# Masking the diagonal exponentials on GpSimd instead of the transposed scores on TensorE, in a causal attention stage

## The reference, cut to what matters

```python
x = x + 0.5 * ffn(layernorm(x))      # 16 experts of 176, top 4, and a shared one of 704
x = x + attention(layernorm(x))      # this case is about this stage
x = x + 0.5 * ffn(layernorm(x))

# attention: 32 query heads, 8 key/value heads, head width 8, rotary positions
scores = jnp.einsum('bhqd,bhkd->bhqk', q, k_rep) / scale
scores = jnp.where((kpos > qpos)[None, None], -jnp.inf, scores)
attn = jax.nn.softmax(scores, axis=-1)
out = jnp.einsum('bhqk,bhkd->bhqd', attn, v_rep)
```

## Time and profile before

| | |
|---|---|
| median of 3 runs | 797.16 us (796.89 to 799.98) |
| the profiled execution | 796.24 us |
| its span, first to last instruction | 794.4 us |
| PE, DVE, ACT, POOL busy over the span | 93%, 58%, 47%, 24% |
| the attention's scores and products | about 283 to 549 us of the span |

### The profile page before, as it was taken

The page is one execution under the profiler, slowest core; times in us unless marked ns, Lnnn a source line. Parts: engine busy times, 40 slices in busy tenths (PEclk is TensorE's granted clock), DMA queues, the critical chain, the costliest instruction groups (busy, mean ns, idle before and its releaser), DMA issues.

```text
span 794.4 us, 13291 instructions
## 1 busy us (share of the span) xinstructions
PE 735.7 (93%) x4776; PEld 391.3 (49%) x4776; DVE 460.9 (58%) x942; ACT 373.9 (47%) x569; POOL 189.7 (24%) x158
## 2 busy tenths in 40 slices
PE   4699999999996677999999999997879999999997
PEld 2356666656564233333333434543446656556665
DVE  6555454545548977899988877643533333333334
ACT  6434343333334466746657667776622222222222
POOL 1273333333344412000000000000143333333332
PEclk9999999999998689999999999999699999999999
DMA  5353333334310000000000000000042222221212
GB/s 170 101 148 112 119 119 113 113 120 133 116 54 1 0 1 1 1 1 1 1 2 1 1 1 2 1 1 1 2 112 77 67 65 72 60 79 53 79 53 80
DMA packets 16169, 44.37 MB, mean 56 GB/s; under 512 B 2658, under 2 KB 5090, under 8 KB 16132
## 3 DMA queue, kind: packets, MB, share of 16 engines
q1 hardware_dynamic: 12388, 33.65, 14.4%
q10 hardware_dynamic: 3744, 10.23, 3.9%
HBM read 42.68 MB, written 1.19 MB: 55 GB/s over the span
## 4 chain that ended last, share of the span: by engine, by line
PE 82%; DVE 6%; issue 4%; ACT 4%; DMA 2%; POOL 1%; SPq 1%; DVEq 0%; ACTq 0%; POOLq 0%
PE psum L857 53%; PE psum L1021 8%; PE psum L1005 8%; PE psum L994 7%; PE psum L992 2%; PE psum L1008 2%; DVE m_part L807 2%; PE psum L979 1%; ACT kT L563 1%; PE psum L1028 1%; DMA coef_dram<-oT 1%; POOL R L379 1%; DVE kaug L797 1%; DMA R<-coef_dram 1%; DMA x_res<-x_dram 1%
## 5 line engine op out<-in xcount | busy, mean ns | idle before, releaser
L857 PE MATMUL psum<-xT,W_hi 128*128 128x512 f16 x880 | 265.2, 383 | 0.0
L379 POOL TENSOR_TENSOR R<-R 128x512 f32<-128x512 f32 x112 | 152.5, 1363 | 298.0 <-DVE R L718 250.1
L807 DVE TENSOR_REDUCE m_part<-psum 128x1 f32<-128x512 f32 (+3 forms) x384 | 188.1, 550 | 42.3 <-PE psum L994 40.1
L704 DVE SCALAR_TENSOR_TENSOR R<-psum,R 128x512 f32<-128x512 f32 x108 | 74.7, 691 | 226.0 <-ACT R L491 225.9
L491 ACT ACTIVATE R<-psum 128x512 f32<-128x512 f32 x108 | 64.4, 597 | 265.5 <-PE psum L857 265.5
L857 PE MATMUL psum<-W_hi,R 128*128 (+1 forms) x896 | 166.5, 275 | 11.5 <-DVE R L718 11.5
L578 ACT ACTIVATE R<-psum 128x1024 f32<-128x1024 f32 x144 | 141.8, 1024 | 68.1 <-PE psum L1005 45.6
L857 PE MATMUL psum<-xT,W_lo 128*128 128x512 f16 x440 | 168.2, 382 | 0.0
L857 PEld LDWEIGHTS psum<-xT,W_hi 128*128 (+1 forms) x880 | 86.8, 99 | 83.4 <-issue 3.5
L857 PE MATMUL psum<-W_lo,R 128*128 (+1 forms) x448 | 123.3, 275 | 0.0
L994 PE MATMUL psum<-kT,qT 128*128 128x512 f16 (+3 forms) x384 | 105.8, 334 | 1.0 <-DVE m_part L807 0.6
(11 more groups left out here) (101 smaller groups left out, 457.3 us busy)
## 6 DMA issues: line engine op xcount, KB each, us to landing
R<-coef_dram SPq DMA_DIRECT2D x64, 256.0 KB, 3.8
w_stage<-w_dram ACTq DMA_DIRECT2D x26, 384.0 KB, 2.9
R<-coef_dram SPq DMA_DIRECT2D x8, 448.0 KB, 3.5
R<-coef_dram SPq DMA_DIRECT2D x8, 384.0 KB, 3.4
R<-coef_dram SPq DMA_DIRECT2D x8, 320.0 KB, 3.5
R<-coef_dram SPq DMA_DIRECT2D x8, 192.0 KB, 3.7
x_res<-x_dram SPq DMA_DIRECT2D x8, 128.0 KB, 2.2
R<-coef_dram SPq DMA_DIRECT2D x8, 128.0 KB, 3.1
```

Of the source, the lines that this page charges most:

```text
L379: nc.gpsimd.tensor_tensor(hc[:, c, :], v[:, j, c, :], C[:, j, c * CH:(c + 1) * CH], ALU.mult).then_inc(s_hc[c], 1)
L704: nc.vector.scalar_tensor_tensor(out=v[:, j, c, :], in0=bank[2 + c][:, :], scalar=1.0 / WS, in1=sg[:, c, :], op0=ALU.mult, op1=ALU.mult).t ...
L807: nc.vector.tensor_reduce(m_part[:, h, kc:kc + 1], ps[:, 0:n], axis=AX.X, op=ALU.max).then_inc(free_of(e), 1)
L857: ins = nc.tensor.matmul(o, stat(a, k), mov(b, k), start=first and n == 0, stop=last and n == 3 * k_parts - 1, **kw)
```

## The change

Line 1008 goes: the transposed scores on the diagonal get no mask. GpSimd gets 32 operations, one for each pair of the 16 diagonal steps, that write zero over the forbidden entries of the exponentials in place. They stand behind the eight bias additions in its program. The diagonal step's `pv` waits for the two of its unit. The planner's cost of a diagonal `st` loses 0.45 on PE and gains 2.5 on GpSimd, so that it writes another order. The mask of the plain scores (line 992) stays.

```diff
         if kind == "st":
             diag = e[5] == ORDER[e[6]]
-            return [(PE, 0.9 if diag else 0.45), (ACTE, 0.95)], [("q2", e[3]), ("st", e[1] - 1, e[2])]
+            return [(PE, 0.45), (ACTE, 0.95)] + [(POOL, 2.5)] * diag, [("q2", e[3]), ("st", e[1] - 1, e[2])]
...
+        s_select = sem("s_select")
...
                 nc.gpsimd.tensor_tensor(x_res[:, t, :], x_res[:, t, :], bias[:, QKV:QKV + D],
                                         ALU.add).then_inc(s_xb, 1)
+
+            for e in events:
+                if e[0] == "st" and e[5] == ORDER[e[6]]:
+                    n, pair = e[1], e[2]
+                    pool.wait_ge(s_exp, 2 * n + pair + 1)
+                    own = prob[:, n % 2, 2 * pair:2 * pair + 2, :].rearrange("p g (j q) -> p (g j) q", q=P)
+                    nc.gpsimd.affine_select(out=own, in_=own, pattern=[[0, 2 * GQ], [1, P]], compare_op=ALU.is_ge,
+                                            fill=0.0, base=0, channel_multiplier=-1).then_inc(s_select, 1)
             low_parts(2)
...
                         ins = nc.tensor.matmul(bank[gl], kT[:, gh * GLO + gl, kt * P:(kt + 1) * P],
-                                               qT2[:, u % 4, :, :], start=True, stop=kt != t)
-                        if kt == t:
-                            ins = nc.tensor.matmul(bank[gl].rearrange("p (j n) -> p j n", j=GQ), identb[:],
-                                                   maskb[:, 1, :].unsqueeze(1).to_broadcast([P, GQ, P]),
-                                                   start=False, stop=True)
+                                               qT2[:, u % 4, :, :], start=True, stop=True)
                     ins.then_inc(s_st, 1)
...
                     pe.wait_ge(s_exp, 2 * n + 2)
+                    if kt == t:
+                        pe.wait_ge(s_select, 2 * (u + 1))
```

## The result

The changed kernel takes 811.83 us (median of 4, 810.75 to 812.35) against 797.77 for the kernel before; the ratio is 1.0167, 95% interval 1.0148 to 1.0185. It is 13 to 14 us slower. The forecast was 801, the range 789 to 813. The sign was right and the size under a third of the real one (0.5% against 1.67%).

The account below looks back on a forecast made before the run. TensorE was taken to bound the attention, VectorE close behind. Masks -13.0, first wait +6.5, other selects +0.5 and +7.5, VectorE +3.5 gave +5.0 on 796.24: 801 us, range 789 to 813.

Parts of the forecast that it names:

- What VectorE takes back: Between 301 and 530 us, TensorE's reduced work brings it close to VectorE's pace: +3.5 us, between 0 and 9.5.
- seven to eighteen: Plain scores counted between a diagonal step's scores and product in units 1 to 10, said to cover the select waits.
- The select's price: One GpSimd select over 1024 fp32 elements per partition: taken as 1.8 us, between 0.9 and 2.7.
- a sign of being wrong: The prediction said it would be wrong if the selects were below 1.1 us.
- dear selects: Rival: selects on GpSimd cost 2.5 to 2.7 us, as for two reads; 812.5 us, +16; chance 0.25.
- The first wait: Product of n = 2 waits for selects queued behind GpSimd's eight bias additions: +6.5 us.
- s: GpSimd's time for one select, taken as 1.8 us.
- Units 1 to 10 covered, 11 to 15 short of 7.5 us: Select waits at diagonal products: hidden in units 1 to 10 but for +0.5 us at unit 10; +7.5 in 11 to 15.
- the formula: Time needed from a diagonal step's first scores to its product, 1.15 + 2s, set against TensorE's work in that stretch.
- Masks at 13.0 us: Dropping the diagonal mask matmuls on TensorE, 60 of 64 counted as saving at 0.216 us each: -13.0 us.
- masks off the path: Rival: VectorE's reduces pace the stretch and 9.5 us is given back; +11, 807 us; chance 0.08.
- TensorE's 98.8%: TensorE busy 98.8 of 100 us between 350 and 450, taken as evidence that it bounds the attention.

Follow-up runs that it names:

- the halved reduces: VectorE's plain-score reduces over half their columns, masks in, no selects: 791.35 us in the order of before, 802.15 us in the new order.
- the two other lists: The changed kernel with the bias additions behind the selects of n = 5 and the planner told 1.1 or 0 us for a select: 800.48 and 794.19 us.
- 0 in the planner: The changed kernel, bias additions behind the selects of n = 5, planner told 0 us for a select instead of 2.5: 794.19 us, ratio 0.9963.
- the kernel without selects: The kernel before, in its old order, with line 1008's masks left out and nothing in their place: 793.65 us, ratio 0.9949.
- the kernel with selects: The changed kernel with the planner's old costs, so the old order, masks out and selects in: 800.48 us, ratio 1.0027.
- the kernel with the additions behind: The changed kernel, same order, with the eight GpSimd bias additions moved behind the selects of n = 5: 806.52 us, ratio 1.0105.

## Why the prediction was wrong

- **The new order, which stood in the sum with nothing of its own.** This is the step that failed. "What VectorE takes back: +3.5 us" was to hold all that the planner's new list does, and it counted only sums of work over 228 us. It held two things. The first, masks that bring less because VectorE stands next to TensorE: in the changed kernel's order they brought 11 us and not 13.0, which the term covers. The second, the new list itself: 18.8 us with masks in, 12 without. I had even used the crowding as a benefit: the "seven to eighteen" plain scores before a diagonal product were what hid the select. I did not ask what the steps look like from which they were taken. Part of the answer stood in the trace of before, where in units 6 to 9 steps with three and with six plain scores take nearly the same time.
- **The select's price.** I took 1.8 us between 0.9 and 2.7; it is 1.094, near the memset's end and under the 1.1 that I had named as a sign of being wrong. My own sum with 1.094 gives some 794 us, on the wrong side. The sign came out right for a reason that I had not priced, and that the time lies in the range is luck too: the upper end was that of dear selects.
- **The first wait**, forecast 6.5 us (5.0 at s = 1.094): the queue behind the additions was there, with 5.4 us on the product; moving them gives 5 us in the new order and 6.7 in the old one. Right in place and nearly in size.
- **Units 1 to 10 covered, 11 to 15 short of 7.5 us.** No product waited for a select in units 1 to 10, but that of n = 55 came 1.0 us later for VectorE's instruction beside the selects. In units 11 to 15 the formula gives 2.3 us at s = 1.094, and the selects cost 2.6. That agreement is luck in part: 1.9 of the 2.6 are at n = 67, where the formula has nothing, since it knew only waits of products.
- **Masks at 13.0 us** would have been wrong in the order of before, where they brought 4.1. The rival "masks off the path", 0.08, holds there in the main; in the changed order it does not, and it priced no order.
- **The evidence of TensorE's 98.8%** misled me. Doubling the masks cost in full and dropping them saved a third: the busy share told that TensorE had no room for more, not that less would help.

What stays open: of the order's 18.8 us the halved reduces take some 8 away; that the other 11 come from the heaps is read from the step times and supported by the two other lists, but not proved, since those lists differ in more than the heaps. A planner that caps the plain scores per step was not tried, nor the masks left out together with halved reduces. What sets the least time of a step (two exponentials of 0.97 us and the waits between scores and products would fit) was not tried either. Why 0 in the planner gives a better end than 1.1 is read from one trace each.

## What to carry to other kernels

Where a cost table or planner orders the work, changing one of its numbers is an edit of its own: run the old work in the new order and the new work in the old order before judging the operation. In a list that was balanced between two engines, as here, adding to one can cost in full and removing from it gain little, so the chain's share of an item bounded its gain from above only. Filler spread evenly among the steps cost little here, and the same filler heaped before a wait did not. An operation that has moved to an idle engine also stands in that engine's queue, and it can lengthen what runs on another engine beside it: compare durations, not only waits.

## What the runs showed of the hardware

- GpSimd's select over 128 x 1024 fp32 in place takes 1092 to 1097 ns in the changed kernel, 1.07 ns an element, against 2.66 for two streams of fp32 in the earlier trace rows. The Trainium skill (GPSIMD Engine Reference, Engine selection) says that one-input operations there run "roughly line-rate". The trace agrees, roughly: the memset, which only writes, has 0.86 ns an element.
- VectorE's instructions that read two tiles of SBUF took 1.03 and 1.23 us beside a pair of selects, and 0.23 and 0.43 us in the same order without selects.
- The clock around a pause changes with little. In the order of before, with the masks in, TensorE kept 2.4 GHz from 296 to 304 us. With the masks out it fell to 1.2 GHz from about 298 us on in the kernel without selects (the product there took 1.94 us for 1.06), and stayed at 2.4 to the end of the scores of n = 2 in the kernel with selects. What decides between the two is not shown. The kernel with the additions behind, which does not wait, has the lower clock there as well.
